# Expert results of the first mixture: stored in slot order by SyncE, gathered by slot on GpSimd

## The reference, cut to what matters

```
# x: 4096 tokens of 256 (16 x 256 of them); w1, w3: 256 x 512; w2: 512 x 256
# W1e, W2e: 8 experts of 256 x 256; all in f32
shared = silu(xf @ w1) * (xf @ w3) @ w2
s = sigmoid(concat([xf, tf]) @ router_W)              # 8 scores for each token
_, topk_idx = top_k(s + router_bias, 2)
gates = s_sel / (s_sel.sum(axis=1) + 1e-9)            # s_sel: s at topk_idx
h = gelu(einsum('nc,ech->enh', xf, W1e))
y = einsum('enh,ehc->enc', h, W2e)
routed = einsum('ne,enc->nc', combine, y)             # combine: gates at topk_idx
out = (shared + routed) / 3
```

## Time and profile before

| | |
|---|---|
| runs | 3079.36, 3078.48, 3076.69 us |
| median | 3078.48 us |
| the profiled execution | 3076.07 us, its span 3074.3 us |
| granted TensorE clock, mean over it | 0.972 |
| TensorE matmul busy | 2874.0 us (93% of the span) |
| TensorE weight loads | 2210.5 us (72%) |
| VectorE busy | 1924.1 us (63%) |
| ScalarE busy | 1202.0 us (39%) |
| GpSimd busy | 482.3 us (16%) |

### The profile page before, as it was taken

How to read it: one execution, slowest core, us unless ns; L and a number is a source line. 1 busy time by engine, 2 the same in 40 slices (tenths; PEclk the granted TensorE clock), 3 DMA queues, 4 the chain that set the end, 5 groups by cost and what they waited for, 6 DMA issues and landing times.

```text
span 3074.3 us, 72493 instructions
## 1 busy us (share of the span) xinstructions
PE 2874.0 (93%) x28542; PEld 2210.5 (72%) x28542; DVE 1924.1 (63%) x6596; ACT 1202.0 (39%) x2713; POOL 482.3 (16%) x615
## 2 busy tenths in 40 slices
PE   8788988999999999999999999978999858999998
PEld 4677457777777777777777777645666638999998
DVE  4444467777777777777777777465677654444444
ACT  1222232333433333343333433234555514555554
POOL 0665000000000000000000000012333212333333
PEclk9889998999999999999999999999999968999999
DMA  3323500101101010010101001111222132222222
GB/s 137 115 86 101 213 23 5 33 22 33 36 22 33 23 33 29 26 36 23 33 22 33 31 27 33 34 37 40 67 74 61 47 107 46 36 38 39 35 39 32
DMA packets 91874, 148.90 MB, mean 48 GB/s; under 512 B 19168, under 2 KB 74464, under 8 KB 88320
## 3 DMA queue, kind: packets, MB, share of 16 engines
q1 hardware_dynamic: 70944, 106.91, 10.5%
q0 software_dynamic: 20448, 37.32, 5.7%
q10 hardware_dynamic: 144, 0.03, 0.0%
HBM read 95.93 MB, written 48.27 MB: 47 GB/s over the span
## 4 chain that ended last, share of the span: by engine, by line
PE 86%; DVE 7%; ACT 2%; issue 2%; DMA 1%; another core or an unknown queue 1%; SPq 0%; POOLq 0%; DVEq 0%; ACTq 0%
PE ps L997 15%; PE ps L816 14%; PE ps L2047 8%; PE ps L1062 8%; PE ps L2062 8%; PE ps L1031 4%; PE ps L978 4%; PE ps L417 3%; PE ps L263 2%; PE ps L428 2%; PE ps L264 2%; PE ps L846 2%; PE ps L847 2%; PE ps L275 2%; PE ps L1539 1%
## 5 line engine op out<-in xcount | busy, mean ns | idle before, releaser
L816 PEld LDWEIGHTS ps<-arena 128*128 128x128 f32 x4096 | 537.6, 193 | 30.1 <-ACT arena L824 3.3
L997 PE MATMUL ps<-arena 128*128 128x256 f32 x2048 | 550.4, 392 | 1.9 <-DVE arena L1007 1.0
L816 PE MATMUL ps<-arena 128*128 128x128 f32 x4096 | 540.6, 276 | 2.9 <-ACT arena L824 2.9
L997 PEld LDWEIGHTS ps<-arena 128*128 128x128 f32 x2048 | 354.8, 190 | 163.5 <-issue 133.3
L824 ACT ACTIVATE arena<-ps 128x256 f32<-128x256 f32 x512 | 196.0, 383 | 546.5 <-PE ps L816 546.1
L1062 PE MATMUL ps<-arena 128*16 128x256 f32 x4096 | 271.5, 383 | 10.5 <-DVE arena L1092 9.9
L1780 POOL MEMSET arena<- 128x3072 f32 x1 | 2.7, 2659 | 1702.6 <-PE ps L997 1702.6
L2047 PE MATMUL ps<-arena 128*128 128x128 f32 x2272 | 267.7, 276 | 0.7 <-DVE arena L2119 0.7
L2047 PEld LDWEIGHTS ps<-arena 128*128 128x128 f32 x2272 | 261.7, 193 | 1.2 <-DVE arena L2119 1.1
L2062 PE MATMUL ps<-arena 128*128 128x256 f32 x1136 | 256.8, 379 | 0.0
L1083 DVE SCALAR_TENSOR_TENSOR arena<-arena 128x128 f32<-128x128 f32 x256 | 73.8, 288 | 281.4 <-ACT arena L1074 281.3
(11 more groups left out here) (286 smaller groups left out, 4739.1 us busy)
## 6 DMA issues: line engine op xcount, KB each, us to landing
xw_scratch<-arena SPq DMA_DIRECT2D x32, 512.0 KB, 2.7
arena<-xw_scratch SPq DMA_DIRECT2D x256, 64.0 KB, 2.7
arena<-in_W SPq DMA_DIRECT2D x16, 1024.0 KB, 5.2
arena<-ys_scratch SPq DMA_DIRECT2D x16, 512.0 KB, 5.0
xn_scratch<-arena SPq DMA_DIRECT2D x32, 129.0 KB, 2.7
arena<-in_xT SPq DMA_DIRECT2D x8, 512.0 KB, 8.8
arena<-in_kinT SPq DMA_DIRECT2D x1, 4096.0 KB, 17.0
arena<-in_xtb SPq DMA_DIRECT2D x32, 128.0 KB, 2.3
```

Source lines behind the costliest of these rows:

```text
L816: m = e.matmul(bank(b)[:, 128 * i:128 * i + 128], kin[:, k, 2 * jp + i, :], xcT[:, k, 128 * blk:128 * blk + 128], start=(k == 0), stop=(k ...
L997: m = e.matmul(bank(7)[:, 0:256], G[blk % 2][:, j, :], kout[:, j, :], start=(j == 0), stop=(j == 31))
```

## The change

Three things are changed together:
- The store of a block is a plain DMA of 128 KB on SyncE (`expert_store_sync`) into rows 128 n to 128 n + 127 of `ysd`. So `ysd` is in slot order and has 9088 rows.
- GpSimd issues the 71 gathers of x in one run (`AHEAD` is gone). Gather n waits for the landing of gather n - 8, and from n = 32 on for the transposes of block n - 32, whose buffer it takes.
- SyncE's 16 row loads are gone. In their place GpSimd waits for all stores to land and for VectorE's last weight copies, and then issues `rows_gpsimd` for chunks 0 to 7: eight indirect DMAs each, 128 rows by `slot`, into the same places of `ya`. Chunk n >= 4 waits for the transposes of chunk n - 4. They count on the semaphores `xs0` to `xs7`, which the weighing waits for.

```diff
@@ -54,7 +54,7 @@
         x2d = out
         xnd = nc.dram_tensor("xn_scratch", [N + 128, D + 2], f32, kind="Internal").ap()
         xwd = nc.dram_tensor("xw_scratch", [2, 128, 1024], f32, kind="Internal").ap()
-        ysd = nc.dram_tensor("ys_scratch", [2 * N + 9216, D], f32, kind="Internal").ap()
+        ysd = nc.dram_tensor("ys_scratch", [9088, D], f32, kind="Internal").ap()
         take = arena.take
 
         def take_at(at, *dims, dt=None):
@@ -217,7 +217,6 @@
         we_at = arena.at
         W1e, W2e = take(8, 512), take(8, 512)
         ya = [take_at(we_at + 2048 * (m // 4 % 4) + 512 * (m % 4), 2, 256) for m in range(32)]
-        ya4 = [take_at(we_at + 2048 * (i % 4), 8, 256) for i in range(8)]
         arena.at = max(arena.at, WORDS - 7744 + 2304)
         route_tab_at = arena.at
         Wa1, Wa2 = [take(2, 256) for _ in range(2)], [take(2, 256) for _ in range(2)]
@@ -225,7 +224,7 @@
         NYA = 8
         ayb = [take(256) for _ in range(NYA)]
         assert arena.at <= WORDS - 256
-        NXA, AHEAD = 32, 10
+        NXA = 32
         axs = [axs_[:, i] for i in range(NXA)]
         a_oh = take_at(after_a + 8192, 4, 8, 256, dt=f16).rearrange("p g t (n s) -> p g t n s", s=2)
         lgT = take_at(after_a + 12288, 2, 512)
@@ -469,23 +468,32 @@
                 e.wait_ge(s[f"xs{n % 8}"], 16 * (n // 8))
             row_gather_gpsimd(e, axs[n % NXA], xtb2, tok[:, n:n + 1], s[f"xs{n % 8}"])
 
-        def expert_store_gpsimd(e, n):
+        def expert_store_sync(e, n):
             e.wait_ge(s["a_y"], n + 1)
-            e.indirect_dma_start(ysd, bass.IndirectOffsetOnAxis(ap=dst[:, n:n + 1], axis=0), ayb[n % NYA], None
-                                 ).then_inc(s[f"ys{n % NYA}"], 16)
+            e.dma_start(ysd[128 * n:128 * n + 128], ayb[n % NYA]).then_inc(s[f"ys{n % NYA}"], 16)
+
+        def rows_gpsimd(e, n):
+            if n >= 4:
+                e.wait_ge(s["c_tr"], 2 * n - 6)
+            for m in range(4 * n, 4 * n + 4):
+                for k in range(2):
+                    row_gather_gpsimd(e, ya[m][:, k], ysd, slot[:, k, m:m + 1], s[f"xs{n}"])
+
+        def rows_count(n):
+            return 16 * uses(NBK, n, 8) + 128
 
 
 
         def weigh_scalar(e, n):
             e.wait_ge(s["rg"], 12)
-            e.wait_ge(s[f"in{n}"], 48)
+            e.wait_ge(s[f"xs{n}"], rows_count(n))
             for m in range(4 * n, 4 * n + 4):
                 x = e.activation(ya[m][:, 0], ya[m][:, 0], ACT.Copy, scale=g12[:, 0, m:m + 1])
             x.then_inc(s["ym"], 1)
 
         def weigh_vector(e, n):
             e.wait_ge(s["ym"], n + 1)
-            e.wait_ge(s[f"in{n}"], 48)
+            e.wait_ge(s[f"xs{n}"], rows_count(n))
             for m in range(4 * n, 4 * n + 4):
                 x = e.scalar_tensor_tensor(ya[m][:, 0], ya[m][:, 1], g12[:, 1, m:m + 1], ya[m][:, 0], ALU.mult, ALU.add)
             x.then_inc(s["cb"], 1)
@@ -661,20 +669,15 @@
 
         def moe1_gpsimd(e):
             e.wait_ge(s["iv"], 24)
-            for n in range(AHEAD):
+            for n in range(NBK):
                 expert_load_gpsimd(e, n)
-            for n in range(NBK):
-                expert_store_gpsimd(e, n)
-                if n + AHEAD < NBK:
-                    expert_load_gpsimd(e, n + AHEAD)
-
-        def rows_sync(e, i):
-            if i >= 4:
-                e.wait_ge(s["c_tr"], 2 * i - 6)
-            for k in range(2):
-                r0 = N * k + 512 * i
-                e.dma_start(ya4[i].rearrange("p (m k) d -> p m k d", k=2)[:, :, k],
-                            ysd[r0:r0 + 512].rearrange("(m p) d -> p m d", m=4)).then_inc(s[f"in{i}"], 16)
+            for i in range(NYA):
+                e.wait_ge(s[f"ys{i}"], 16 * uses(NBK, i, NYA))
+            e.wait_ge(s["a_w1"], NBK)
+            e.wait_ge(s["a_w2"], NBK)
+            for n in range(8):
+                e.wait_ge(s[f"xs{n}"], 16 * uses(NBK, n, 8))
+                rows_gpsimd(e, n)
 
         def moe1_sync(e):
             e.dma_start(xT[:, :, 0:512], I["xT"][:, :, 0:512]).then_inc(s["in0"], 16)
@@ -703,12 +706,8 @@
             e.wait_ge(s["iv_mm"], 1)
             e.dma_start(wq, I["wq"]).then_inc(s["wqk"], 16)
             e.dma_start(kT, I["keysT"]).then_inc(s["wqk"], 16)
-            for i in range(NYA):
-                e.wait_ge(s[f"ys{i}"], 16 * uses(NBK, i, NYA))
-            e.wait_ge(s["a_w1"], NBK)
-            e.wait_ge(s["a_w2"], NBK)
-            for i in range(4):
-                rows_sync(e, i)
+            for n in range(NBK):
+                expert_store_sync(e, n)
             e.wait_ge(s["a_tr"], NBK)
             e.dma_start(kin, I["kinT"]).then_inc(s["kin"], 16)
             e.wait_ge(s["a_dn"], NBK)
@@ -716,8 +715,6 @@
             e.dma_start(lbr, I["lb"]).then_inc(s["wx"], 16)
             e.dma_start(h0, I["h0T"]).then_inc(s["wx"], 16)
             e.dma_start(Wh, I["Wh"]).then_inc(s["wx"], 16)
-            for i in range(4, 8):
-                rows_sync(e, i)
             e.wait_ge(s["kc_mm"], 4)
             e.dma_start(kout[:, 10:32], I["kout"][:, 10:32]).then_inc(s["kout"], 16)
             e.wait_ge(s["sh_dn"], 16)
@@ -1646,7 +1643,7 @@
         def norm2_gpsimd(e, q):
             for m in (2 * q, 2 * q + 1):
                 e.wait_ge(s["po_h"], m + 1)
-                e.wait_ge(s[f"in{m % NXB}"], 16 * (m // NXB + 4))
+                e.wait_ge(s[f"in{m % NXB}"], 16 * (m // NXB + 2))
                 e.tensor_tensor(xb[m % NXB], xb[m % NXB], hx[:, m], ALU.add).then_inc(s["po_x2"], 1)
             if q < 14:
                 e.wait_ge(s["po_gu"], gu_count(q))
...
```

More of the change, by code:

```diff
@@ L1727, in xo_count @@
         def xo_count(m):
-            return 48 + 16 * (m // NXB + 1)
+            return 16 * (m // NXB + 2)
         def xb_load_sync(e, q):
@@ L1992, in xs_count @@
         def xs_count(n):
-            return 16 * uses(NBK, n % NX, 8) + 16 * (n // NX + 1)
+            return rows_count(n % NX) + 16 * (n // NX + 1)
         def route_tensor(e):
```

## The result

Over 20 runs of each, the changed kernel took 3084.53 us in the median (3078.59 to 3091.09) and the kernel before 3076.43 us (3070.79 to 3080.67): a ratio of 1.0023, 95% interval 1.0017 to 1.0030. Forecast was 3058.5 us, so the change is slower by 8 us where 20 us less were expected. The experiments will show that this answer holds on some chips only; on another the same change gains 1.06%.

What follows compares the result with a forecast made beforehand. TensorE bounds the kernel; in the expert stage its completions come late while GpSimd issues indirect DMAs back to back. Expert stage -35 and shared layer +15 give -20: 3076.1 to 3056, plus 2.4 for the median, 3058.5 us; range 3022 to 3090.

Steps and rivals of the forecast that it cites:

- The bound and the clue: Expert stage: TensorE's completions reach other engines late while GpSimd issues indirect DMAs back to back, 5.64 us a block.
- Item 1: Expert stage: moving 71 stores from GpSimd to SyncE halves GpSimd's work there and costs nothing.
- Item 2: Start of expert stage: back-to-back gathers up to 32 ahead, 5.64 us a block until about 135 us, losing about 5 blocks.
- Item 3: Rest of expert stage: 63 blocks at 1.98 us plus 2 us for low clock, ending at 262 not 297: -35 us.
- Item 4: Shared layer: 64 row gathers, 82 us, hidden as data by TensorE's matmuls; chunk 7 late from 1.49 us a gather.
- Item 5: Shared layer: back-to-back row gathers make TensorE's completions late, mainly for keys and transposes: +15 us, from 0 to +24.
- A late completion costs 0.7 us a matmul: Shared layer: 5.64 us a block over 8 f32 matmuls, less than the layer's own 512-column matmuls of 0.86 us.
- the whole of TensorE's work is stretched: Rival: back-to-back issue slows all TensorE work by 2.85, adding 53 us beside the shared layer: +18, 3096; chance 0.13.
- Every DMA counts: Rival: stores on SyncE delay TensorE too, blocks stay at 2.94 us, shared layer adds 0 to 24: 3090; chance 0.12.
- rows late: Rival: GpSimd's issues held up to 1.57 us, shared layer waits 24 us for chunk 7: +4, 3082; chance 0.02.
- Nothing is given back: Rival: no late completions in the shared layer: -35, 3043; with harmless first gathers too, -68, 3010; chance 0.33.
- The rule weighed: Gathers beside VectorE's f32 copies: at worst 0.24 us more each, no term, against the skill's about 3100 ns a DMA.

Runs made afterwards that it cites:

- e7: Changed kernel, gathers of x ten blocks ahead and eight memsets after every eighth gather by slot: 3013.84 us, ratio 0.9798 to the kernel before.
- e6: Changed kernel, unedited, on a chip where the kernel before took 3074.69 us: 3083.32 us, ratio 1.0029.
- e18: Changed kernel, unedited, on a chip where the kernel before took 3041.29 us: 3009.18 us, ratio 0.9894.
- e16: Changed kernel with two small memsets after every gather, of x and by slot: 3018.74 us, ratio 0.9813 to the kernel before.
- e11: Changed kernel with one small memset after each gather of x, gathers by slot replaced by plain GpSimd loads: 3046.14 us, ratio 0.9902 to the kernel before.
- e12: Changed kernel with eight memsets after every 16th gather of x, gathers by slot replaced by plain SyncE loads: 3049.86 us, ratio 0.9913 to the kernel before.
- e15: Changed kernel with gathers by slot fetching only 64 of 256 columns: 3087.84 us, ratio 1.0035 to the kernel before.

## Why the prediction was wrong

- **The bound and the clue: right.** On the late chips, close indirect DMAs of GpSimd make TensorE's completions late, in both stages (e7 against e6). What the prediction did not ask is whether a delay seen on one chip belongs to the kernel or to the chip: on a prompt chip the same kernel has none (e18).
- **Item 1 (stores by SyncE cost nothing): right.** From 138.6 us on, blocks stand at 1.98 us with a store each.
- **Item 2 (the first gathers): the mechanism right, the size off.** At 1.25 us a gather a block took 17.6 and 21.8 us, not 5.64; four blocks were through at 135.4 us, not eight.
- **Item 3: right.** From there 1.98 us a block; step 3 began at 268 us, forecast 262, and the stage gave 29 us of the 35. The 2 us for the low clock were not needed: from 135 us on it was 0.99.
- **Item 4 (rows as data are hidden): right** at 1.25 us a gather: in the shared layer no engine waits for a DMA of rows. e16 shows the other side at 1.63, beyond the 1.49 that the item worked out.
- **Item 5 is the step that failed.** It priced the gathers beside the shared layer at +15 us; they cost 40 in the profiled run and 30 in e6's, which more than eats up the 29 us of item 3. "A late completion costs 0.7 us a matmul" was taken as a constant, and on it rested the claim that the layer's own matmuls of 0.86 us hide the delay. In the expert stage it was 3.5 us a matmul, and in the shared layer the long matmuls' results were late too: the one with w3 issued at 285.81 us reached VectorE at 314.51. That each costs 3.5 us there is not shown. The 0.7 was probably a lower bound: the 4.21 us of the earlier trace rows end at 183.42 us, as GpSimd's run of issues ends (183.54) after 10 us, so the end of the run may have cut the delay off. In the changed kernel the delay starts only 10 us into a run, and the runs last 46 and 40 us.
- **The delay against the spacing, late chips.** Blocks come 2.86 us apart at 2.86 / 2 = 1.43 us a DMA in the kernel before, 4.35 at 1.44 and 5.7 to 8.6 at 1.36 in e11, about 28 (8 x 3.5, an estimate) at 1.25, and nothing is late beside the shared layer at a mean of 1.57 (e7) and at 1.63 (e16). The two values near 1.44 differ, so spacing alone does not give the delay.
- **The rivals.** By its mechanism "the whole of TensorE's work is stretched" came nearest: 3096 worked out, 3085 measured. Its factor, 2.85, was too small for the late stretches; that its 53 us were still too much fits the harmless first 10 us of each run, of which there are three beside the shared layer, since the waits for transposes split the gathers into 32, 16 and 16 (argued, not tested). "Every DMA counts" (3090) and "rows late" (3082) lie nearer in number, by chance: the first fell with e12 and with the 71 stores of item 1, the second with the gathers of 949 ns. "Nothing is given back" with harmless first gathers, 3010, is what a prompt chip gives: 3009.18.
- **The rule weighed.** 64 gathers beside the shared layer's VectorE work took 945 to 1108 ns, not the 3100 that the Trainium skill ("SBUF — State Buffer", "SBUF: two separate sides") has for its case. The times here are the issuing instruction's, and the skill's is a DMA's beside one VectorE copy, so they are not the same measure; no run showed GpSimd held up.

## What to carry to other kernels

A delay read off a trace belongs to the load and to the length of the stretch that it was read in. If the change makes such stretches longer or closer, give the term a range of its own, look whether the end of the stretch cut the delay off, and compare how steeply the trace's own stretches differ. Where TensorE works beside GpSimd's indirect DMAs, keep these about 1.6 us apart in the mean, by waits that are there anyway (ten blocks ahead) or by a short pause after every eight. In this kernel it cost nothing that could be measured on prompt chips (3008 to 3011 against 3009) and gave 2.3% on a late one. And time a change on more than one chip before its sign is believed.

## What the runs showed of the hardware

- The same program has two speeds: before 3039.5 to 3044.4 on four chips, 3074.69 to 3077.87 on three, each chip at one time only. The stretches behind the first mixture do not differ: the LSTM's weight loads (L813) span 1519.3 us in e18 and 1519.7 in the profile after.
- On the late chips completions of TensorE reach the other engines late while GpSimd issues indirect DMAs 1.25 us apart, from about 10 us into such a run on: 3.5 us for each f32 matmul in the profile after, 4.0 in e6 and e15. They are made good within 6 us of the last issue.
- What these contend for was not found. It is not the bytes (e15), not SyncE's traffic (e12), and not plain DMAs by GpSimd, as far as 17 us of them show (e11).
- Why the kernel before gains 35 us on a prompt chip is only argued (a pair of 2.57 us or less would bound it); no profile of it was taken there.
